# Cross attention and a quantised feed-forward in one program: the down weights are made by VectorE from whole numbers and zeros, and the loads get a written-out order

## What is computed

```python
x = x + xattn(layernorm(x), ctx, ctx, Wq, bq, Wk, bk, Wv, bv, Wo, bo)   # 8 heads, softmax over the 64 rows of a block
x = x + ffn(layernorm(x), gate_w, gate_z, gate_s, up_w, up_z, up_s, down_w, down_z, down_s)

def dequantize(imatrix, scales, zeros):          # group size 128 along the rows of the matrix
    return (imatrix - repeat(zeros, 128)) * repeat(scales, 128)

gate = silu(x @ dequantize(gate_w, gate_s, gate_z))      # gate_w, up_w: int32, 512 x 1792
up = x @ dequantize(up_w, up_s, up_z)
return (gate * up) @ dequantize(down_w, down_s, down_z)  # down_w: int32, 1792 x 512
```

## Time and profile before

| | us |
|---|---|
| median of 3 runs | 432.85 (430.18 to 434.37) |
| the profiled execution, its time | 432.93 |
| its span (first to last instruction) | 431.1 |
| TensorE busy | 408.5 (95%) |
| ScalarE, VectorE, POOL busy | 320.9, 317.9, 259.2 |

### The profile page before, as it was taken

One profiled execution on the slowest core, in us unless ns is written; L12 is line 12 of the kernel. 1 busy time (PEld: TensorE's weight loads), 2 busy tenths in 40 slices (PEclk: granted clock), 3 DMA queues, 4 the chain that ended last, 5 costly groups with the idle time before them and its releaser, 6 DMA issues.

```text
span 431.1 us, 10671 instructions
## 1 busy us (share of the span) xinstructions
PE 408.5 (95%) x4228; PEld 317.5 (74%) x4228; DVE 317.9 (74%) x564; ACT 320.9 (74%) x529; POOL 259.2 (60%) x273
## 2 busy tenths in 40 slices
PE   5888899969999999999999999999999999999994
PEld 3756678747877777777777877777877888888872
DVE  4788448559787768788887677787887667667676
ACT  2327798647878788777688888687788998988970
POOL 3434598499776745575464854764566555555561
PEclk8899999989999999999999999999999999999999
DMA  6798999999950010002000000000000000001003
GB/s 217 168 225 161 302 287 263 263 264 244 247 91 24 2 27 2 26 2 75 27 27 26 2 1 25 27 2 26 26 27 0 2 2 17 9 24 50 0 0 98
DMA packets 27526, 35.60 MB, mean 83 GB/s; under 512 B 2606, under 2 KB 19158, under 8 KB 27478
## 3 DMA queue, kind: packets, MB, share of 16 engines
q1 hardware_dynamic: 17490, 23.79, 17.3%
q0 software_dynamic: 9360, 11.01, 15.5%
q10 hardware_dynamic: 628, 0.14, 0.2%
HBM read 30.65 MB, written 4.28 MB: 81 GB/s over the span
## 4 chain that ended last, share of the span: by engine, by line
PE 75%; DVE 8%; DMA 5%; issue 4%; ACT 3%; SPq 2%; POOL 2%; POOLq 0%; DVEq 0%; ACTq 0%
PE banks L721 21%; PE banks L723 19%; PE banks L734 10%; PE banks L735 10%; DMA wd<-z_out 4%; PE banks L619 3%; PE banks L659 2%; DVE yT L985 2%; PE banks L648 2%; PE banks L637 2%; PE banks L629 2%; SPq L268 1%; PE banks L678 1%; DVE st L882 1%; DMA xn<-in_L_ffn_down_s 1%
## 5 line engine op out<-in xcount | busy, mean ns | idle before, releaser
L515 ACT ACTIVATE banks<-banks,ratio 128x512 f32<-128x512 f32 x336 | 208.0, 662 | 39.2 <-PE banks L723 29.2
L985 DVE SCALAR_TENSOR_TENSOR yT<-banks,sd,yT 128x512 f32<-128x512 f32 x208 | 154.4, 747 | 53.5 <-PE banks L735 52.8
L721 PE MATMUL banks<-xT,wgu 128*128 128x512 f32 x448 | 182.4, 407 | 1.4 <-DVE t_sb L973 1.2
L723 PE MATMUL banks<-xT,wgu 128*128 128x512 f32 x448 | 175.5, 392 | 0.0
L378 POOL TENSOR_TENSOR t_sb<-t_sb,u_sb 128x512 f32<-128x512 f32 x56 | 76.6, 1368 | 60.6 <-DVE t_sb L973 60.5
L721 PEld LDWEIGHTS banks<-xT,wgu 128*128 128x128 f32 x448 | 84.3, 188 | 22.6 <-DVE t_sb L973 2.4
L723 PEld LDWEIGHTS banks<-xT,wgu 128*128 128x128 f32 x448 | 84.5, 189 | 15.4
L734 PE MATMUL banks<-hr,wd 128*128 128x512 f32 x224 | 89.6, 400 | 5.8 <-DVE yT L985 3.9
L735 PE MATMUL banks<-hr,wd 128*128 128x512 f32 x224 | 87.8, 392 | 0.0
L391 POOL TENSOR_TENSOR hr<-t_sb,hr 128x512 fp32r<-128x512 f32 x56 | 72.2, 1290 | 5.1 <-ACT hr L537 0.7
L734 PEld LDWEIGHTS banks<-hr,wd 128*128 128x128 f32 x224 | 42.2, 188 | 20.7 <-DVE yT L985 11.3
(11 more groups left out here) (91 smaller groups left out, 364.8 us busy)
## 6 DMA issues: line engine op xcount, KB each, us to landing
wgu<-z_out SPq DMA_DIRECT2D x14, 512.0 KB, 16.6
x_sb<-in_x SPq DMA_DIRECT2D x16, 256.0 KB, 12.0
out<-x_sb SPq DMA_DIRECT2D x16, 256.0 KB, 2.2
wgu<-in_L_ffn_gate_w POOLq DMA_DIRECT2D x7, 512.0 KB, 10.2
wgu<-in_L_ffn_up_w POOLq DMA_DIRECT2D x7, 512.0 KB, 9.9
wd<-z_out SPq DMA_DIRECT2D x7, 512.0 KB, 12.2
wd<-in_L_ffn_down_w POOLq DMA_DIRECT2D x7, 512.0 KB, 10.4
ctx_sb<-in_ctx SPq DMA_DIRECT2D x12, 256.0 KB, 3.7
```

The costliest lines, as they stand in the source:

```text
L515: act.activation(banks[:, bank, :], banks[:, bank, :], ACT.Copy, scale=ratio[:, m, g, it:it + 1]).then_inc(done[n % 2], 1)
L721: pe.matmul(banks[:, bank, :], w, xT[:, c % 2, 0, g, :], start=g == 0, stop=False, skip_group_check=True)
L723: pe.matmul(banks[:, bank, :], w, xT[:, c % 2, 1, g, :], start=False, stop=True, skip_group_check=True).then_inc(full[n % 2], 1)
L985: dve.scalar_tensor_tensor(y, bank, sd[:, it, b:b + 1], y, ALU.mult, ALU.add).then_inc(s_free, 1)
```

## The change

Gate and up weights are still made by loading zeros and adding the whole numbers in a DMA, now under the semaphores `s_zgu` and `s_wgu`, and with POOL issuing its ten adds of the loop after other places (`add_after`). The down weights are made otherwise: SP loads the whole numbers of a pair of blocks as they are (`wd_in`, int32, at the same SBUF place as `wd`), loads the whole-number zeros of the pair straight from `down_z` into all partitions (`z_d`, in one of two slots that lie in `yT1`, the sum of the second chunk, unused till then), and VectorE subtracts (`less_zeros`, one instruction of 128x512 for each of the 14 blocks, at places 8i+4 and 8i+5). The seven down adds leave POOL, and a third of `z_out` is gone. TensorE waits for the subtractions (`s_dif`). A load of zeros into a slot waits on SP until the subtraction of two pairs before is done. SP's order of loads is written out line by line; the first four gate and up zeros go out together.

The core of the diff (lines of `-` and `+` that only rename are left out with "..."):

```diff
-    EARLY = 4
-    piece_after = {q: EARLY + i for i, q in enumerate((0, 2, 4, 8, 9, 12, 15, 16, 19, 21, 24, 26, 28, 31, 33, 36, 38))}
...
+    NB = NI // 2
+    add_after = {0: 4, 3: 5, 8: 6, 11: 7, 16: 8, 19: 9, 24: 10, 27: 11, 32: 12, 35: 13}
+
+    sub_after = {8 * i + 4 + half: (i, half) for i in range(NB) for half in range(2)}
...
+        with ExitStack() as s1:
+            wd_in = sb("wd_in", [P, NI, L], I32, s1)
         wd = sb("wd", [P, NI, L], F32R)
...
+        z_d = yT1.rearrange("p (j i) r -> p j i r", j=2).bitcast(I32)
...
-            CTX_AT = {9: PRE + 2, 11: PRE + 3, 15: PRE + 4, 18: PRE + 5}
...
+            def load_down(i):
+                b = slice(2 * i, 2 * i + 2)
+                sync.dma_start(wd_in[:, b, :], down_w[2 * i * P:(2 * i + 2) * P, :].rearrange(
+                    "(g p) n -> p g n", p=P)).then_inc(s_wd[i], 16)
+                if i >= 2:
+                    sync.wait_ge(s_dif, 2 * (i - 1))
+                sync.dma_start(z_d[:, i % 2, :, :], down_z[b, :].partition_broadcast(P)).then_inc(s_zd[i % 2], 16)
...
-            load_zeros(0)
-            load_zeros(1)
-            for k in range(2, EARLY + 1):
-                (load_ctx if k % 2 else load_x)(PRE + (k - 2) // 2)
-                sync.wait_ge(s_w[k - 2], 16)
                 load_zeros(k)
-            load_ctx(PRE + 1)
-            for k in range(EARLY + 1, NP):
-                load_zeros(k)
-                if k in CTX_AT:
-                    load_ctx(CTX_AT[k])
-                if k < EARLY + 1 + NT - PRE - 2:
-                    load_x(PRE + 1 + k - EARLY)
+            load_x(4)
+            load_ctx(4)
+
+            sync.wait_ge(s_wgu[1], 16)
+            load_x(5)
+            load_down(0)
+            sync.wait_ge(s_wgu[2], 16)
+            load_ctx(5)
+            load_zeros(4)
+            load_zeros(5)
+            load_x(6)
+            sync.wait_ge(s_wgu[3], 16)
+            load_zeros(6)
+            load_zeros(7)
+            load_ctx(6)
+            load_down(1)
+            load_zeros(8)
+            load_zeros(9)
+            load_x(7)
+            load_down(2)
+            load_ctx(7)
+            load_zeros(10)
+            load_zeros(11)
+            load_down(3)
+            load_x(8)
+            load_zeros(12)
+            load_zeros(13)
+            load_down(4)
+            load_ctx(8)
+            load_x(9)
+            load_down(5)
+            load_ctx(9)
+            load_x(10)
+            load_down(6)
+            for t in range(11, NT):
+                load_x(t)
...
-                if q in piece_after:
-                    add_weights(piece_after[q])
+                if q in add_after:
+                    add_weights(add_after[q])
...
-                        wait_weights(pe, "d", 0, it // 2)
+                        pe.wait_ge(s_dif, n + 2)
...
+            def less_zeros(i, half):
+
+                dve.wait_ge(s_wd[i], 16)
+                dve.wait_ge(s_zd[i % 2], 16 * (i // 2 + 1))
+                b = 2 * i + half
+                dve.tensor_tensor(wd[:, b, :], wd_in[:, b, :], z_d[:, i % 2, half, :], ALU.subtract).then_inc(s_dif, 1)
...
+                if q in sub_after:
+                    less_zeros(*sub_after[q])
```

More of the change, by code:

```diff
@@ L139, in xattn_ffn @@
         yT = [yT0, yT1]
-        z_raw, z_neg = (yT0[0:NG * I // 64, b, 0:3 * 64].rearrange("p (m n) -> p m n", m=3) for b in range(2))
+        z_raw, z_neg = (yT0[0:NG * I // 64, b, 0:2 * 64].rearrange("p (m n) -> p m n", m=2) for b in range(2))
+        z_d = yT1.rearrange("p (j i) r -> p j i r", j=2).bitcast(I32)
         with ExitStack() as s3:
@@ L180, in xattn_ffn @@
         ri = sb("ri", [P, 2 * NC])
-        z_out = nc.dram_tensor("z_out", [3, NG * I], F32)
+        z_out = nc.dram_tensor("z_out", [2, NG * I], F32)
         banks = keep.enter_context(nc.psum_tensor("banks", [P, 8, 512], F32))
@@ L192, in xattn_ffn @@
         s_ctx = [sem(f"s_ctx{i}") for i in range(2)]
-        s_w = [sem(f"s_w{k}") for k in range(NP)]
-        s_z = [sem(f"s_z{k}") for k in range(NP)]
-        s_zraw, s_zneg, s_zout = sem("s_zraw"), sem("s_zneg"), sem("s_zout")
+        s_wgu = [sem(f"s_wgu{k}") for k in range(2 * NB)]
+        s_zgu = [sem(f"s_zgu{k}") for k in range(2 * NB)]
+        s_wd = [sem(f"s_wd{i}") for i in range(NB)]
+        s_zd = [sem(f"s_zd{i}") for i in range(2)]
+        s_zraw, s_zneg, s_zout, s_dif = sem("s_zraw"), sem("s_zneg"), sem("s_zout"), sem("s_dif")
         s_tr, s_tr2, s_trs, s_wT, s_prep, s_scl, s_low, s_brow, s_bqk = (
@@ L251, in freed_for, with gu_piece @@
             return s - 1 if s < wide else min(s - 1, wide) if s < wide + 4 else s - 3
[L253 to L258, removed]
+        def gu_piece(k):
+            i, m = divmod(k, 2)
+            return wgu[:, m, :, 2 * i * P:(2 * i + 2) * P]
         def flat(a):
@@ L278, in load_zeros @@
             def load_zeros(k):
[L279 to L284, removed]
-            CTX_AT = {9: PRE + 2, 11: PRE + 3, 15: PRE + 4, 18: PRE + 5}
+                i, m = divmod(k, 2)
+                z = z_out[m].rearrange("(g n) -> g n", g=NG)[:, 2 * i * P:(2 * i + 2) * P]
+                sync.dma_start(gu_piece(k).bitcast(F32), z.partition_broadcast(P)).then_inc(s_zgu[k], 16)
+            def load_down(i):
[5 more added lines that the diff above has]
+                sync.dma_start(z_d[:, i % 2, :, :], down_z[b, :].partition_broadcast(P)).then_inc(s_zd[i % 2], 16)
             sync.dma_start(wraw[:, 1, :], Wk).then_inc(s_wsm, 16)
@@ L302, in _ @@
             sync.wait_ge(s_zout, 16)
-            load_zeros(0)
-            load_zeros(1)
-            for k in range(2, EARLY + 1):
-                (load_ctx if k % 2 else load_x)(PRE + (k - 2) // 2)
-                sync.wait_ge(s_w[k - 2], 16)
-                load_zeros(k)
-            load_ctx(PRE + 1)
-            for k in range(EARLY + 1, NP):
-                load_zeros(k)
-                if k in CTX_AT:
-                    load_ctx(CTX_AT[k])
-                if k < EARLY + 1 + NT - PRE - 2:
-                    load_x(PRE + 1 + k - EARLY)
+            for k in range(4):
+                load_zeros(k)
+            load_x(4)
[33 more added lines that the diff above has]
+                load_x(t)
             for c in range(1, NCH):
@@ L363, in add_weights @@
             def add_weights(k):
[L365 to L372, removed]
+                i, m = divmod(k, 2)
+                pool.wait_ge(s_zgu[k], 16)
+                pool.dma_start(gu_piece(k), (gate_w, up_w)[m][:, 2 * i * P:(2 * i + 2) * P].rearrange(
+                    "(g p) n -> p g n", p=P), accum_op=ALU.add).then_inc(s_wgu[k], 16)
             def product(n):
@@ L411, in _ @@
             raised()
+            add_weights(2)
             weigh(1)
             rstd(1, 0)
-            add_weights(2)
+            add_weights(3)
             weigh(2)
@@ L456, in _ @@
             load(s_wsm2, wraw[:, 3, :], Wo)
-            for m, z in enumerate((gate_z, up_z, down_z)):
+            for m, z in enumerate((gate_z, up_z)):
                 load(s_zraw, z_raw[:, m, :].bitcast(I32), z.rearrange("g (a n) -> (g a) n", n=64))
@@ L539, in _ @@
             norm1(0)
[L540 removed]
+            act.wait_ge(s_zraw, 32)
             act.activation(z_neg, z_raw.bitcast(I32), ACT.Copy, scale=-1.0).then_inc(s_zneg, 1)
@@ L981, in take_down @@
                 if it == 0:
+                    if n == NI and b == 0:
+                        dve.wait_ge(s_dif, 2 * NB)
                     dve.tensor_scalar(y, bank, sd[:, it, b:b + 1], None, ALU.mult).then_inc(s_free, 1)
```

15 lines of the change are left out of this document (2 added, 13 removed).

## The result

| | median us | lowest to highest | runs |
|---|---|---|---|
| kernel before | 432.96 | 429.93 to 436.72 | 20 |
| changed kernel | 434.65 | 433.55 to 436.36 | 20 |

The ratio is 1.0041, with a 95% interval from 1.0023 to 1.0059. The forecast was 428.7 us with a range of 426.3 to 433.0; it missed by 6 us, and in direction. The interval leaves 1 out, so the changed kernel is slower, by 0.4%; by the bound of 1% that the prediction set, the change made no difference. The profiled execution took 434.65 us, its span is 432.7 us.

The account below looks back on a forecast made before the run. The prediction took TensorE's own work to bound the kernel nearly everywhere, with only one dip in chunk 0 able to give time back. Sum: 432.93 − 5.5 + 0.6 + 0.7 = 428.7 us, range 426.3 to 433.0.

Parts of the forecast that it names:

- Prologue: nothing: Ahead of the loop: `z_neg` waits for two loads instead of three, the chain does not run through it; no cost.
- The stall at places 19 to 22: −5.5: Chunk 0: POOL no longer waits for zeros there, `rstd` is on time, the stall goes; −5.5 us.
- the dip: TensorE's slowdown in chunk 0, 82.35 to 94.54 us: costs 5.5 us, 3.3 idling and 2.2 half clock and restart.
- The first gate: +0.6: Pair 0's second subtraction lies straight ahead of `gated(0)`, which TensorE already awaits; on the path in full, +0.6 us.
- The other twelve subtractions: +0.7: VectorE in chunk 0: mostly hidden by the slack of two banks, two more small waits; +0.7 us, bounds 0 and 7.8.
- New waits on the down pairs: nothing: VectorE at places 8i+4: whole numbers and zeros land in time while landings stay below 22.7 us; no cost.
- Late down weights: Rival: down weights reach VectorE late at 8i+4, each stop costs 5.5 us; two give 439.7 us; chance 0.10.
- the dip stays: Rival: other zeros late for POOL, or place 22's `rstd` waits for something else; 434.2 us, chance 0.06.
- Shared access: Rival: VectorE's subtractions and POOL's SBUF operations wait for each other, 0.5 us each; 431.0 us, chance 0.20.
- more comes back: Rival: the small waits go as well and the subtractions hide; 426.5 us, chance 0.14.

Follow-up runs that it names:

- Experiment 2: Changed kernel with the prologue's loads and adds of zeros in the order of the kernel before: 433.97 us, ratio 1.0012.
- experiments 7: Changed kernel, zeros in the old order, first down pair issued behind the zeros of piece 7: 439.5 us; the same with subtractions spread: 436.51 us.
- experiment 9: Changed kernel, zeros in the old order, first down pair loaded late, subtractions spread, those of pair 0 at places 7 and 9: 429.72 us, ratio 0.9930.
- Experiment 4: Kernel before with the changed kernel's prologue: first four zeros together, adds 2 and 3 earlier; 430.41 us, ratio 0.9947.
- experiments 2, 4 and 5: The last of the three: both kernels traced once more without any edit; one profiled execution each, 431.62 us (before) and 435.0 us (changed).
- experiment 6: Both kernels with TensorE's idle-time matmuls ahead of the loop lengthened from 3 to 15 blocks: before 431.83 us, changed 437.37 us.
- Experiment 1: Changed kernel with its fourteen subtractions spread to other places, none straight ahead of a gate: 431.91 us, ratio 0.9974.
- experiment 3: Kernel before with the adds of places 19 and 21 moved behind places 22 and 23: 431.11 us, ratio 0.9958.

## Why the prediction was wrong

The forecast of 428.7 us was 5.95 us too low, and two terms of its sum share that almost evenly: the prologue, put at nothing, cost 3.84 − 1.20 = 2.64 us, and the twelve subtractions, put at 0.7, cost 3.67, which is 2.97 more. The first was a mechanism that the prediction didn't have; the second was there and too small.

**Prologue: nothing.** This is the step whose mechanism failed. Its words were "`z_neg` waits for two loads instead of three; the chain does not run through it, so nothing". No stop of TensorE ahead of the loop is put down to that chain in the trace. But the new order puts four broadcasts of zeros together at 12 us, and the first down pair at 31 us, on the DMA engines that also bring TensorE's instructions. The blocks came 3.2 us later, and gate_up with them: +3.84 us, less the 1.2 us of an "issue" wait at 47.84 us that went. Experiment 2 against experiments 7 and 9 shows both halves of it: apart zeros bring the second block back, a late down pair the fourth, and with both the start came back. Experiment 4, which has no down pair in the prologue, shows that zeros together are enough to make it late. A late down pair with the zeros together was not run. The stops are the cause, and after the longer ones (1.68 to 2.67 us in experiments 2, 4 and 5) the granted clock fell to half for a while, which is part of the price. The order of loads stood in the diff, and the trace of before had TensorE wait 1.03 and 1.01 us for "issue" at 26.96 and 47.84 us. I costed the moved loads by who waits for their data, and not by what passes through the same engines.

The Trainium skill (Runtime: NRT & Kernel Launch, § Instruction fetch mechanics) says that each sequencer brings its program by a DMA queue of its own in blocks of 16 KiB, and that the cost of crossing a boundary is "mostly hidden". The packets of q8 agree with the first. The second holds in the loop, where the longest such wait is 1.0 us; in the prologue, with the engines at a share of 1.0 and more, a boundary cost up to 2.67 us.

**The stall at places 19 to 22: −5.5.** Right. TensorE's drift over it is −5.37 us, POOL waits for no zeros after 20 us, no `rstd` is late, and no wait of over 1.4 us is left in chunk 0. In the changed kernel alone the cause isn't separated, since the dip also goes with a late start and with the new start of experiment 4; experiment 9 shows that it goes with an early start too. What the sum didn't see is what the stall did for the kernel: by experiment 6 it took up 3.0 us of lateness ahead of it. Taken alone, −5.5 and a late prologue would both be paid for; in the kernel before the new prologue costs 5.0 us and gives 6.8 back in chunk 0 (experiment 4).

**The first gate: +0.6.** Right: +0.64 us, and TensorE waits 1.14 us there, where 1.0 was said.

**The other twelve subtractions: +0.7.** Too small by a factor of five: +0.58, +1.24, +0.65 and +1.20, together 3.67 us, within the bounds of 0 and 7.8. I read VectorE's load over the whole chunk (84%) and took the rest for slack. What counts is the instruction that stands right behind, and whether TensorE already waits for it: at 57.5, 99.6 and 143.9 us a subtraction fell just ahead of such a gate, and TensorE paid for it, with waits of 1.14, 1.08 and 1.32 us. The one at 113.43 us also stands straight ahead of a gate and cost nothing; the drift stays at −0.12 us there. Experiment 1, with the same 14 subtractions elsewhere, is 2.9 us faster.

**New waits on the down pairs: nothing.** Right for the order as written: whole numbers and zeros landed in 7.7 and 6.9 us in the median, and no subtraction waited. Experiments 7 and 9 show how little was in hand: issued 17 us later, the first pair cost 4.7 to 7.1 us.

**The rivals.** "Late down weights" and "the dip stays" didn't happen. "Shared access" did, small. The subtractions of the changed kernel, and the pair of instructions where it cost most:

```profile
L975 DVE TENSOR_TENSOR wd<-wd_in,yT x14: 675/684/1506, 53.1 to 143.9; 128x512 fp32r<-128x512 int32 x14
```

```profile
95.89 1.51 DVE L975 TENSOR_TENSOR wd<-wd_in,yT 128x512 fp32r<-128x512 int32 x1
```

```profile
95.80 1.04 POOL L374 TENSOR_TENSOR e_sb<-e_sb,ri 128x512 f32<-128x512 f32 x1
```

Minimum, median and maximum are in ns. POOL began 0.09 us earlier and ended at 96.84; the subtraction ended 0.56 us after that. The Trainium skill's rule (SBUF — State Buffer, § Who interferes with whom) says that the one that comes second waits for the first, and this pair agrees with it. Where the subtraction came first, POOL's took longer: at 57.72 us `rs` took 0.99 instead of 0.55 us. But only four of the fourteen were lengthened, by 1.3 us in all, where the rival had reckoned with half a microsecond for each. Experiment 1 says that this is not what cost: there ten of the fourteen took over 0.75 us, 4.6 us more than 684 ns each in all, and that kernel is 2.9 us faster. So the 3.67 us are in the main a matter of place. How much of them comes from the four longer ones isn't shown. And "more comes back" was the reverse of what came.

The sum with what was measured: 432.93 + 3.84 − 1.20 + 0.64 − 5.37 + 3.67 = 434.5 us, against 434.65. With both failed terms mended (experiment 9) the kernel took 429.72 us, 1 us above the forecast.

## What to carry to other kernels

Loads that are moved or bunched are to be costed by all that shares the DMA engines with them, TensorE's instruction blocks too: look in the trace for "issue" waits in the middle of a loop of matmuls, and at the instruction queue beside them. A stall that waits for DMAs can hide lateness ahead of it; before booking its removal, ask what will then count, and try a deliberate delay, which shows it in one run. And work added to a busy engine is to be costed place by place, by what stands right behind it and what waits for that, not by the engine's share.

## What the runs showed of the hardware that was not expected

Whenever TensorE had broken off in mid-loop, it went on 1.2 to 1.6 us after the end of a 16 KB packet of the instruction queue, in both kernels and in all variants that show such a stop.

A clock of 1.00 in a row is not always a measured one. In the changed kernel the row of 17 to 22 us reads 1.00:

```profile
17.00:22.00 5.00, 4.82 (x122) 3.84 (x126) 2.14 (x7) 1.39 (x2) 3.50 (x5) 1.00 1.08 305
```

```profile
17.18 1.13 PE L640 MATMUL banks<-wT,xn 64*64 64x64 f32 x32 [0.70 <-DVE qkT L921]
```

Yet these 32 matmuls took 1.13 us. The clock records of this trace begin only at 23.1 us, and where there is none the row shows 1.00. In experiment 2 the same group also took 1.13 us, and there the records are complete: the row of 8 to 22 us reads 0.51:

```profile
8.00:22.00 14.00, 11.96 (x287) 9.45 (x283) 10.05 (x24) 4.09 (x8) 5.30 (x7) 0.51 0.76 187
```

```profile
16.87 1.13 PE L642 MATMUL banks<-wT,xn 64*64 64x64 f32 x32 [0.70 <-DVE qkT L923]
```

In the kernel before such a group takes 0.69 us at 24.32 us, at full clock. The rise from 1.2 to 2.4 GHz came at 14.7 us in the trace of before, and by the durations at about 23 us in the changed kernel. Where the block was late anyway the half clock ahead of it cost little: the one trace of the changed kernel (half clock to 23 us) and the other (full clock, then a wait of 2.55 us for the block) start gate_up at 48.66 and 48.90 us.

The half clock that comes after a stop is another matter. TensorE stood 2.67, 2.55 and 1.68 us for a block in experiments 4, 5 (the changed kernel) and 2, and 3.28 us in the dip of the kernel before. In each case the granted clock went to half within 1.6 us of the moment when it went on, and stayed there for 10.2, 3.5, 3.4 and 3.4 us. After the wait of 1.99 us in experiment 3 it did not fall.
